# The second layer of a recurrent network, rewritten batch by batch without engine loops

## What is computed

```python
x1 = x0 + s * silu(state)                       # state with half of its features shifted by one token
xm = (x1 - mean(x1)) / sqrt(var(x1) + 1e-5)
# causal attention over 512 tokens, one head of 128
q, k, v = rotate(xm @ Wq.T), rotate(xm @ Wk.T), xm @ Wv.T
att = softmax(where(key <= query + 1, q @ k.T / sqrt(128), -inf)) @ v
# eight adapters of width 64, the two best of each token
logits = xm @ w_gate
gates = softmax over the two largest logits, 0 elsewhere
hidden = relu(xm @ Wd[e] + bd[e])
moe = 0.5 * sum_e gates[e] * (hidden @ Wu[e] + bu[e])
out = x1 + att * silu(moe)
```

## Time and profile before

| | us |
|---|---|
| median of 3 runs | 1978.37 (1969.48 to 1980.21) |
| the profiled execution | 1981.07 |
| its span, first to last instruction | 1979.0 |
| TensorE busy | 1831.6 (93%) |
| VectorE busy | 1474.9 (75%) |
| ScalarE busy | 1181.4 (60%) |
| GpSimd busy | 1200.0 (61%) |

### The profile page before, as it was taken

One profiled execution on the slowest core, in us unless ns is written; L12 is line 12 of the kernel. 1 busy time (PEld: TensorE's weight loads), 2 busy tenths in 40 slices (PEclk: granted clock), 3 DMA queues, 4 the chain that ended last, 5 costly groups with the idle time before them and its releaser, 6 DMA issues. The chain is left out here.

```text
span 1979.0 us, 70992 instructions
## 1 busy us (share of the span) xinstructions
PE 1831.6 (93%) x30440; PEld 1160.3 (59%) x30440; DVE 1474.9 (75%) x1658; ACT 1181.4 (60%) x2030; POOL 1200.0 (61%) x1291
## 2 busy tenths in 40 slices
PE   5867999999999999999999999999999999976898
PEld 4744656665666566566656665666566656653444
DVE  5547788888788888878887888888887887843443
ACT  4325576667666666766676667666766666644333
POOL 0118866777677677767776777777667767720000
PEclk9979999999999999999999999999999999987888
DMA  1022322322222323223222223232232222201000
GB/s 48 0 81 69 77 59 57 100 69 70 68 70 66 89 74 77 64 61 98 66 74 67 71 66 90 69 80 70 56 91 68 74 71 60 67 20 48 6 5 11
DMA packets 84769, 125.09 MB, mean 63 GB/s; under 512 B 26208, under 2 KB 31976, under 8 KB 84336
## 3 DMA queue, kind: packets, MB, share of 16 engines
q1 hardware_dynamic: 84464, 120.64, 24.2%
HBM read 21.98 MB, written 1.05 MB: 12 GB/s over the span
## 5 line engine op out<-in xcount | busy, mean ns | idle before, releaser
L317 POOL TENSOR_TENSOR qkn<-t 128x1024 f32<-128x1024 f32 x192 | 453.8, 2364 | 314.2 <-DVE t L720 313.3
L308 POOL TENSOR_TENSOR qkn<-qkn,rn 128x512 f32<-128x512 f32 x384 | 397.8, 1067 | 14.6 <-POOL rn L302 1.3
L444 PEld LDWEIGHTS sc_ps<-prT,v_win 64*64 64x64 f32 x12288 | 197.8, 135 | 147.6 <-issue 146.7
L584 ACT ACTIVATE sq<-qk_ps 128x1024 f32<-128x1024 f32 x192 | 196.0, 1021 | 102.1 <-PE qk_ps L384 99.9
L399 PE MATMUL ring<-ident,qkn 128*128 128x128 f32 x1536 | 242.5, 281 | 10.6 <-POOL qkn L308 9.6
L399 PEld LDWEIGHTS ring<-ident,qkn 128*128 128x128 f32 x1536 | 176.8, 141 | 124.0 <-issue 75.6
L716 DVE TENSOR_TENSOR t<-qk_ps,rot 128x1024 f32<-128x1024 f32 x192 | 229.3, 1194 | 17.0 <-POOL rot L287 8.7
L325 POOL TENSOR_TENSOR pn<-pexp,rden 128x512 f32<-128x512 f32 x192 | 196.5, 1045 | 75.0 <-DVE rden L704 75.0
L720 DVE TENSOR_TENSOR t<-qk_ps,rot 128x1024 f32<-128x1024 f32 x192 | 232.7, 1212 | 0.0
L730 DVE TENSOR_REDUCE sums<-sq 128x16 f32<-128x1024 f32 x192 | 232.1, 1209 | 0.0
L577 ACT COPY prT<-ring 128x512 f32<-128x512 f32 x192 | 111.2, 580 | 201.5 <-PE ring L428 200.8
(11 more groups left out here) (235 smaller groups left out, 2881.7 us busy)
## 6 DMA issues: line engine op xcount, KB each, us to landing
v_win<-v_tok SPq DMA_DIRECT2D x1488, 64.0 KB
wqkv<-in_w_qkv SPq DMA_DIRECT2D x18, 512.0 KB, 3.7
wo<-in_w_o SPq DMA_DIRECT2D x6, 512.0 KB, 3.9
w<-in_w SPq DMA_DIRECT2D x6, 341.0 KB, 3.3
w<-in_w SPq DMA_DIRECT2D x6, 192.0 KB, 3.0
r_xtok<-in_x SPq DMA_DIRECT2D x4, 256.0 KB, 3.9
amask<-in_att_mask SPq DMA_DIRECT2D x1, 1024.0 KB
out_x<-xo SPq DMA_DIRECT2D x4, 256.0 KB, 2.3
```

The costliest lines, as they stand in the source:

```text
L308: nc.gpsimd.tensor_tensor(by_head(quarter(qkn, f)), by_head(quarter(qkn, f)), rn[:, 8 * f:8 * (f + 1)].unsqueeze(2).to_broadcast([P, 8, DH ...
L317: nc.gpsimd.tensor_tensor(half(qkn, k), half(t1, k), half(t2, k), ALU.add).then_inc((q_added, k_added)[k], 1)
L444: ins = nc.tensor.matmul(sc_ps[64 * par:64 * (par + 1), part, P * pair + WIN * q:P * pair + WIN * (q + 1)], v_win[64 * part:64 * (part + 1 ...
```

## The change

`build_second_layer` is written anew.

- The loops over batches are gone. Each engine has one list of calls for all four batches, in which the work of neighbouring batches is interleaved. Preparation is done by batch too.
- PSUM is a ring of five banks for most products (`fills` names their order, `bank_free` the wait before each refill), two banks for scores, one for the attention's output.
- The projections of q and k are one product of 512 columns each, with features on the partitions, so the rotated terms aren't turned back. The sine part is two instructions on half the partitions each. GpSimd adds the two terms (`add_terms`).
- The gate weights stand beside those of v, so the logits are 8 more columns of each value product (136 columns for each token tile).
- Scores and p are made for the key blocks that the mask leaves: 256, 384, 512 and 512 columns.
- The gates aren't spread by a product: SyncE stores the turned gates to DRAM, waits, and loads them with eight DMAs that repeat each row on 64 partitions (`spread_gates`). VectorE adds the bias and multiplies with the gates in one instruction, and ScalarE's relu follows.
- p isn't normalised; the sum's reciprocal is multiplied into the gate branch (`scale_branch`). silu is made from tanh. No call loads a function table explicitly.
- The up products and the attention's output have tokens on the partitions, so the output isn't turned; x1 is (`turn_x1`). GpSimd adds x1 and the product for three batches, VectorE for the last.

New functions and the begin of each engine's list (TensorE from `centre(0)`, ScalarE from `silu(0)`, VectorE from `gated_x1(0)`), indentation cut:

```diff
+fills = [("xc", 0, 0), ("var", 0, 0), ("vg", 0, 0), ("vg", 0, 1), ("qk", 0, 0), ("qk", 0, 1), ("xc", 1, 0), ("var", 1, 0),
+         ("gate", 0, 0), ("vg", 1, 0), ("qk", 1, 0), ("vg", 1, 1), ("down", 0, 0), ("qk", 1, 1), ("down", 0, 1), ("xc", 2, 0),
+         ("gate", 1, 0), ("var", 2, 0), ("down", 0, 2), ("down", 0, 3), ("vg", 2, 0), ("vg", 2, 1), ("up", 0, 0), ("xc", 3, 0),
+         ("qk", 2, 0), ("var", 3, 0), ("down", 1, 0), ("down", 1, 1), ("qk", 2, 1), ("vg", 3, 0), ("gate", 2, 0), ("down", 1, 2),
+         ("up", 1, 0), ("vg", 3, 1), ("down", 1, 3), ("gate", 3, 0), ("qk", 3, 0), ("down", 2, 0), ("qk", 3, 1), ("down", 2, 1),
+         ("down", 2, 2), ("down", 2, 3), ("x1", 0, 0), ("down", 3, 0), ("down", 3, 1), ("x1", 1, 0), ("down", 3, 2), ("up", 2, 0),
+         ("down", 3, 3), ("up", 3, 0), ("x1", 2, 0), ("x1", 3, 0)]
+place = {f: n for n, f in enumerate(fills)}
...
+def bank_free(what, b, c):
+    n = place[what, b, c] - RING
+    if n < 0:
+        return None
+    what, b, c = fills[n]
+    return dict(xc=(xm_there.sem, b + 1), var=(ln_there.sem, b + 1), vg=(v_copied.sem, v_copied.at(b, c + 1)), x1=(x1_copied.sem, b + 1),
+                gate=(g_copied.sem, b + 1), qk=(a_terms.sem, a_terms.at(b, c + 1)), down=(e_hg.sem, e_hg.at(b, c + 1)), up=(e_u.sem, b + 1))[what]
...
+        def spread_gates(b):
+            sp.wait_ge(g_copied.sem, b + 1)
+            sp.dma_start(gate_rows[:, b, :], gaT[:, b, :]).then_inc(g_stored.sem, 16)
+            sp.wait_ge(g_stored.sem, 16 * (b + 1))
+            if b >= 2:
+                sp.wait_ge(e_hg.sem, e_hg.at(b - 2, 4))
+            for e in range(NE):
+                sp.dma_start(spread[BN * (e % 2):BN * (e % 2 + 1), b % 2, e // 2, :],
+                             gate_rows[e:e + 1, b, :].to_broadcast([BN, T])).then_inc(g_spread[b % 2].sem, 16)
...
+        def add_terms(b, k):
+            pool.wait_ge(a_terms.sem, a_terms.at(b, k + 1))
+            if b >= 2:
+                pool.wait_ge(a_sc.sem, a_sc.at(b - 2, TILES))
+            nc.gpsimd.tensor_tensor(aqk[:, b % 2, k, :], aq1[:, b % 2, k, :], aq2[:, b % 2, k, :], ALU.add).then_inc(a_rot.sem, 1)
...
+        def values(b, part):
+            if part == 0:
+                pe.wait_ge(xm_there.sem, b + 1)
+                if b == 0:
+                    pe.wait_ge(c_first.sem, first_done)
+            free("vg", b, part)
+            for t in ((0, 1, 2), (3,))[part]:
+                ins = nc.tensor.matmul(bank_of("vg", b, part)[:, VG * (t % 3):VG * (t % 3 + 1)], tile(xm, b, t), wvg[:, :], start=True, stop=True)
+            ins.then_inc(v_full.sem, 1)
...
+        def project(b, k):
+            if k == 0:
+                pe.wait_ge(xm_there.sem, b + 1)
+                if b == 0:
+                    pe.wait_ge(c_first.sem, first_done)
+            free("qk", b, k)
+            nc.tensor.matmul(bank_of("qk", b, k), wa[:, P * k:P * (k + 1)], xm[:, b, :], start=True, stop=True).then_inc(a_full.sem, 1)
...
+        def scores(b, t):
+            n = TILES * b + t
+            if t == 0:
+                pe.wait_ge(a_rot.sem, a_rot.at(b, 2))
+                if b == 0:
+                    pe.wait_ge(c_bf.sem, 1)
+            if n >= 2:
+                pe.wait_ge(a_pT.sem, n - 1)
+            nc.tensor.matmul(sc[:, n % 2, 0:width(t)], aqk[:, b % 2, 0, P * t:P * (t + 1)], aqk[:, b % 2, 1, 0:width(t)],
+                             start=True, stop=False, skip_group_check=True)
+            nc.tensor.matmul(sc[:, n % 2, P * t:width(t)], ident_bf[:, :], amask_bf[:, 0:width(t) - P * t], start=False, stop=True,
+                             skip_group_check=True).then_inc(a_sc.sem, 1)
...
+        def up(b, c):
+            pe.wait_ge(e_relu.sem, e_relu.at(b, c + 1))
+            to = bank_of("up", b)
+            if c == 0:
+                free("up", b)
+                for t in range(TILES):
+                    nc.tensor.matmul(to[:, P * t:P * (t + 1)], tile(gaT, b, t), bu[:, :], start=(t == 0), stop=False, skip_group_check=True)
+            for t in range(TILES):
+                ins = nc.tensor.matmul(to[:, P * t:P * (t + 1)], hg[:, b % 2, c, P * t:P * (t + 1)], wu[:, c, :], start=False, stop=(c == 3 and t == TILES - 1),
+                                       skip_group_check=True)
+            if c == 3:
+                ins.then_inc(e_up.sem, 1)
...
+        centre(0)
+        variance(0)
+        values(0, 0)
+        values(0, 1)
+        project(0, 0)
+        project(0, 1)
+        centre(1)
+        variance(1)
+        turn_gates(0)
+        values(1, 0)
+        project(1, 0)
+        scores(0, 0)
+        scores(0, 1)
+        values(1, 1)
...
+        def silu(b):
+            for late, rows in enumerate(HALVES):
+                ins = nc.scalar.activation(sgT[rows, b, :], state[rows, b * SHIFTED + late:b * SHIFTED + late + T], ACT.Silu)
+            ins.then_inc(s_gate.sem, 1)
...
+        def deviation(b):
+            act.wait_ge(var_full.sem, b + 1)
+            nc.scalar.activation(xsq[:, b, :], bank_of("var", b), ACT.Ln, bias=eps_col[:, 0:1]).then_inc(ln_there.sem, 1)
+            act.wait_ge(ln_there.sem, b + 1)
+            nc.scalar.activation(rstd[:, b, :], xsq[:, b, :], ACT.Exp, scale=-0.5).then_inc(rstd_there.sem, 1)
...
+        def exponentials(b, t):
+            n = TILES * b + t
+            act.wait_ge(a_neg.sem, n + 1)
+            if n >= 2:
+                act.wait_ge(a_pturn.sem, n - 1)
+            nc.scalar.activation(aex[:, n % 2, 0:width(t)], sc[:, n % 2, 0:width(t)], ACT.Exp, bias=aneg[:, n:n + 1], scale=AK,
+                                 accum_out=aden[:, n:n + 1]).then_inc(a_exp.sem, 1)
...
+        silu(0)
+        silu(1)
+        square(0)
+        deviation(0)
+        copy_values(0, 0)
+        copy_values(0, 1)
+        gate_exp(0)
+        square(1)
+        deviation(1)
+        copy_gates(0)
+        copy_values(1, 0)
+        silu(2)
+        copy_values(1, 1)
+        exponentials(0, 0)
+        exponentials(0, 1)
+        copy_pT(0, 0)
...
+        def rotate_cos(b, k):
+            dve.wait_ge(a_full.sem, a_full.at(b, k + 1))
+            if b >= 2:
+                dve.wait_ge(a_rot.sem, a_rot.at(b - 2, k + 1))
+            nc.vector.tensor_tensor(aq1[:, b % 2, k, :], bank_of("qk", b, k), arot[:, 0, :], ALU.mult)
+        def rotate_sin(b, k):
+            for to, of in (HALVES, HALVES[::-1]):
+                ins = nc.vector.tensor_tensor(aq2[to, b % 2, k, :], bank_of("qk", b, k)[of, :], arot[of, 1, :], ALU.mult)
+            ins.then_inc(a_terms.sem, 1)
...
+        def gated_hidden(b, c):
+            dve.wait_ge(e_down.sem, e_down.at(b, c + 1))
+            if c == 0:
+                dve.wait_ge(g_spread[b % 2].sem, 16 * NE * (b // 2 + 1))
+                if b >= 2:
+                    dve.wait_ge(e_up.sem, b - 1)
+            nc.vector.scalar_tensor_tensor(hg[:, b % 2, c, :], bank_of("down", b, c), bd[:, c:c + 1], spread[:, b % 2, c, :], ALU.add, ALU.mult).then_inc(e_hg.sem, 1)
...
+        def scale_branch(b):
+            dve.wait_ge(e_u.sem, b + 1)
+            dve.wait_ge(a_rden.sem, b + 1)
+            nc.vector.tensor_tensor(u[:, :, :], u[:, :, :], arden[:, TILES * b:TILES * (b + 1)].unsqueeze(2).to_broadcast([P, TILES, P]), ALU.mult).then_inc(u_scaled.sem, 1)
...
+        gated_x1(0)
+        gated_x1(1)
+        normed(0)
+        shift_logits(0)
+        rotate_cos(0, 0)
+        rotate_sin(0, 0)
+        ranks(0)
+        gates(0)
+        rotate_cos(0, 1)
+        rotate_sin(0, 1)
+        normed(1)
+        rotate_cos(1, 0)
+        row_max(0, 0)
+        row_max(0, 1)
+        shift_logits(1)
+        ranks(1)
+        gated_hidden(0, 0)
+        gated_x1(2)
...
```

More of the change, by code:

```diff
@@ L1259, in build_second_layer @@
[L1259 to L1271, removed]
@@ new lines, in _ @@
+                turn_p(0, 0)
+                turn_p(0, 1)
+                down(0, 1)
+                scores(0, 2)
+                scores(0, 3)
+                centre(2)
+                attend(0, 0)
+                turn_gates(1)
+                turn_p(0, 2)
+                variance(2)
+                attend(0, 1)
+                down(0, 2)
+                down(0, 3)
+                turn_p(0, 3)
+                scores(1, 0)
+                attend(0, 2)
+                values(2, 0)
@@ new lines, in _ @@
+                scores(1, 1)
+                values(2, 1)
+                attend(0, 3)
+                up(0, 0)
+                up(0, 1)
+                up(0, 2)
+                up(0, 3)
+                centre(3)
+                turn_p(1, 0)
+                project(2, 0)
+                turn_p(1, 1)
+                variance(3)
+                scores(1, 2)
+                down(1, 0)
+                down(1, 1)
+                scores(1, 3)
+                attend(1, 0)
+                project(2, 1)
@@ new lines, in _ @@
+                deviation(2)
+                copy_pT(0, 3)
+                relu(0, 1)
+                relu(0, 2)
```

(38 more changed lines are left out.)

737 lines of the change are left out of this document (390 added, 347 removed).

## The result

| | before | after |
|---|---|---|
| median of the runs | 1976.95 us (1969.48 to 1980.21) | 1912.87 us (1910.31 to 1914.68) |
| ratio | | 0.968, 95% interval 0.965 to 0.971 |
| profiled execution / its span | 1981.07 / 1979.0 | 1912.28 / 1910.5 |
| the last stage, from its first table load to the end of the span | 178.5 | 115.15 |

The kernel is 64 us faster by the medians, 1912.87 where 1916 was forecast. The two profiled spans differ by 68.5 us, of which 63.3 lie in the stage. The other 5.2 lie ahead of it, in code that the change doesn't touch: the stage began at 1795.35 us here and at 1800.53 before. So the experiments, most of which have one execution, are read by the length of the stage. The changed kernel run again gave 115.0 for it.

What follows compares the result with a forecast made beforehand. TensorE was taken to bound the stage from the first scores on: 27.5 head + 80.3 (74.7 / 0.93) + 4 clock + 4.4 end = 116.2 instead of 178.5 us, so 1916 us against the median; range 1903 to 1940.

Steps and rivals of the forecast that it cites:

- The sum: The last stage's forecast length: 27.5 + 80.3 + 4 + 4.4 = 116.2 us instead of 178.5.
- First scores: End of scores(0, 0), batch 0's first score product on TensorE, put at about 27.5 us into the last stage.
- 4 for the clock: Allowance of 4 us for some 4 us of work at half clock around the start of the attention.
- The end: The stage's close: gated_out 0.7, add_out 0.7, then 2.9 from last write to end of span, 4.4 us.
- The head: Stage start up to the first scores, a chain through the engines: normed batch 0 at 12.4 us, scores at about 27.5.
- Ln's table load: ScalarE's load ahead of batch 0's Ln, put on the path after the variance product, from 7.7 to 9.0 us.
- The table loads: ScalarE's function-table loads in the new stage: 13 at 1.283 us, taken as 17 us, with no drain added.
- The gates' way: From copied to spread gates through DRAM: 8.4 us, bounds 4.6 and 11.5; by the taken value it costs nothing.
- The rival of late gates: Gates taking 11.5 us or more hold VectorE before gated_hidden(0, 0): 3 to 10 us, 1919 to 1926; chance 5%.
- the one on the loops: Loop overhead at batch turns is small: longest issue time 0.33 us, about 1 us for three turns; no gain hangs on it.
- The one on dependence at a clock of 0.85: Dependence between engines binds: TensorE fed 93% or 80% at the old clock, stage 126.4 or 142, 1926 or 1942; chance 30%.
- the slower rival: TensorE's clock stays at 1.2 GHz through gaps every few microseconds: stage sum 192.5 us, whole kernel 1992; chance 2%.

## Why the prediction was right, and where its steps were not

**The sum.** It gave 116.2 us for the stage; it is 115.15. That is 63.3 us less than before, for 62.3 forecast. First scores: 27.5 forecast, 1824.7 - 1795.35 = 29.3 measured. From there 84.3 forecast (80.3 and 4 for the clock), 1906.5 - 1824.7 = 81.8 measured. The end: 4.4 and 4.0. The two large terms missed by about 2 us each in opposite ways; that they cancel is luck.

**The head.** The centring and the variance product took 2.06 and 2.09 us, not the 1.5 and 1.4 that I took from four such products, part of which had run at the high clock. Against that stood Ln's table load: I put it on the path, but the load is queued ahead of the wait and ran beside the variance product, from 1802.21 to 1803.49, so it cost nothing for batch 0. So the prediction's sentence that a load comes after the engine's wait is wrong here: the row on which I leaned shows a load behind a wait, and doesn't show that every load stands there. The normed batch 0 came at 12.4 us, as forecast. The ties took 1.07 us longer beside GpSimd's addition, which no row of before had shown; that addition took 1.49 us. Six of the eight took 1.27 or 1.28 and one 1.77, not 1.07: the row from which I took the price is another operation, a multiplication, and why it is cheaper isn't shown.

**The table loads** are 13 as counted: 4 of Ln, 4 of the deviation's Exp, 3 of silu, 2 of the scores' Exp, 1283 ns each. No drain shows behind them: 1805.06 + 1.28 and Exp at 1806.35.

**The gates' way** took 10.3 us for 8.4, inside the bounds: the store 1.44 (2.3), the issues 0.64 apart (0.47), the last load 4.47 (2.3). VectorE waited 1.1 us ahead of the first gated hidden. The rival of late gates asked for a way of 11.5 us or more, which didn't come; yet the gates were the last to arrive by those 1.1 us, since VectorE was free 33.5 us into the stage and the copied gates came at 24.1, as forecast.

**TensorE from the first scores.** 77.5 of 81.8 us busy is 95%, where 93% was taken from the earlier trace rows. The 4 us for the clock were not needed there; the clock was 1.00 throughout, and all that the low clock cost, 6.4 us, was in the head. The work was priced too low, 87.3 us for 82.8 (the batch's terms as written add up to 20.5 and not 20.7): from the first scores on TensorE had 77.5 us to do and not 74.7. The up products with their bias are a part of it, 4.85 us a batch in the chain for 4.5. So the right total of this part is owed to a clock allowance that covered work. VectorE's 71 us were 70.7; ScalarE's 72 were 65.9, of which the loads are 16.7, and neither bound the stage.

**The step that failed** is the one on the loops. I read the longest issue time at a turn, 0.33 us, and concluded that nothing of the gain hangs on loops. The issue time was right, and the conclusion skipped the clock. Writing out the loops alone takes 10.0 us off the stage before, and 14.4 off it with the causal blocks. The sum didn't suffer, since it priced the new stage from its work and not from the old one less its cuts. How much of the changed kernel's own gain is owed to its missing loops can't be told from it; what it has is a clock of 1.00 where a batch before had 0.85.

**The rivals.** The one on dependence at a clock of 0.85 was wrong for this order and right for the other: batch by batch the stage is 195.5 us. That the slower rival's 192.5 is close to it is luck. Its clock was 0.73, not 0.50, and its idle time 78 us, which that rival didn't have.

What stays open: what in a turn decides how long the clock stays low behind it, 10 us in one kernel, 3.5 in another and anything from none to 13.8 in two more at the same gaps; and how much of the 80 us between the two orders is the clock and how much is waiting. By the table the clock is 117.4 - 88 = 29 against 6, so 23, and waiting 78 - 21 = 57, but one brings the other.

## What to carry to other kernels

Price a rewritten stage engine by engine from its own work, and then ask of the order whether the engine that bounds it ever stops: the same instructions took 115 and 195 us in two orders. A microsecond of idle TensorE, at a loop's turn or anywhere, is to be priced with the slow products that can follow it: here they cost from nothing to 6.7 us a turn. Where a single chain fills the head, idle TensorE time can be spent on products that nobody reads; the stage got 2.7 us shorter by it, which the time of the whole kernel is too unsteady to show. Before a shared table is asked for, every function behind it is to be looked at: here it saved the loads of Exp and brought back loads for tanh.

## What the runs showed of the hardware that was not expected

- Written-out loops shortened a stretch at 1.2 GHz behind each turn from about 10 to 3.5 us, with gaps of 0.69 us for 0.87 to 1.15. With the causal blocks the same gaps had other stretches: 6.8 to 13.8 us with loops, none or 6.8 without.
- With the table for Ln and Exp loaded, tanh needed a load of its own (1283 ns, twice); behind Exp's own table it needed none.
- Useless TensorE work made the stage shorter: 3.6 us more of busy time, 2.7 us less of length.
- A two-input VectorE instruction on 128x256 took 1.49 us beside a GpSimd addition on 128x512, and 0.42 alone; the addition took 1.49 where most others of the same kind took 1.27.
- Eight loads of 128 KB landed the last of a batch's gates 4.47 us after the last issue; two of 512 KB took 8.74. Fewer and larger DMAs were slower in all.
